# Row maxima of four heads as four 32-row matmul tiles in an attention layer between two ternary feed-forward layers

## The reference

```
x = x + 0.5 * ffn(layernorm(x))       # relu(h @ Wq1.T + b1) @ Wq2.T + b2, 512 hidden, weights in {-1, 0, 1}
x = x + attn(layernorm(x))
x = x + 0.5 * ffn(layernorm(x))
def attn(x):
    q, k, v = heads(x @ Wq.T + bq), heads(x @ Wk.T + bk), heads(x @ Wv.T + bv)
    q, k = rope(q, k)
    return concat(softmax(q @ k.T / sqrt(8)) @ v) @ Wo.T + bo
```

## Time and profile before

| | us |
|---|---|
| Time, median of 3 runs | 548.01 (lowest 547.97) |
| The profiled execution | 545.37 |
| Its span in the profile | 543.5 |
| PE busy | 498.4 (92%) |
| DVE busy | 396.5 (73%) |
| ACT busy | 365.1 (67%) |
| POOL busy | 219.8 (40%) |

### The profile page before, as it was taken

The page is one execution under the profiler, slowest core; times in us unless marked ns, Lnnn a source line. Parts: engine busy times, 40 slices in busy tenths (PEclk is TensorE's granted clock), DMA queues, the critical chain, the costliest instruction groups (busy, mean ns, idle before and its releaser), DMA issues.

```text
span 543.5 us, 8687 instructions
## 1 busy us (share of the span) xinstructions
PE 498.4 (92%) x3230; PEld 234.4 (43%) x3230; DVE 396.5 (73%) x579; ACT 365.1 (67%) x432; POOL 219.8 (40%) x291
## 2 busy tenths in 40 slices
PE   5777988899999999999999999999899999998986
PEld 4455633433444435353535333533344433432445
DVE  3773976768887697768877788778876887888224
ACT  4659866577657685768566866687576757675751
POOL 1553646136554363437351645155513631103202
PEclk7897999999999999999999999999899999999999
DMA  7138026402540247003710444034501470000000
GB/s 225 47 104 240 4 67 190 98 22 98 143 93 2 56 159 159 1 26 114 197 39 6 126 141 103 2 96 154 124 1 50 167 156 2 22 1 3 2 21 19
DMA packets 19177, 44.60 MB, mean 82 GB/s; under 512 B 2624, under 2 KB 5440, under 8 KB 18112
## 3 DMA queue, kind: packets, MB, share of 16 engines
q1 hardware_dynamic: 18464, 43.53, 29.2%
q10 hardware_dynamic: 672, 0.52, 0.3%
HBM read 20.45 MB, written 18.87 MB: 72 GB/s over the span
## 4 chain that ended last, share of the span: by engine, by line
PE 72%; DVE 12%; ACT 10%; issue 3%; DMA 1%; POOL 1%; SPq 0%; ACTq 0%; DVEq 0%; POOLq 0%
PE heads_acc L556 21%; PE unit L541 13%; PE unit L526 11%; PE side L611 8%; DVE maxima L837 8%; ACT probs L747 5%; PE side L594 3%; PE side L599 3%; PE side L605 3%; PE heads_acc L619 2%; ACT hidden L737 2%; PE side L580 2%; DVE x_lo L854 2%; PE unit L611 1%; PE side L590 1%
## 5 line engine op out<-in xcount | busy, mean ns | idle before, releaser
L837 DVE TENSOR_REDUCE maxima<-unit 128x2 f32<-128x1024 f32 x256 | 303.4, 1221 | 72.3 <-PE unit L526 70.7
L747 ACT ACTIVATE probs<-unit 128x1024 f32<-128x1024 f32 x256 | 254.5, 1024 | 99.7 <-PE unit L541 98.3
L556 PE MATMUL heads_acc<-probs,v_heads 128*32 128x512 f32 x1024 | 136.7, 607 | 1.1 <-ACT probs L747 1.1
L541 PE MATMUL unit<-q_stack,k_stack 64*128 64x512 f32 x512 | 113.8, 463 | 8.3 <-DVE maxima L837 4.8
L526 PE MATMUL unit<-k_stack,q_stack 62*128 62x512 f32 x512 | 106.5, 438 | 6.9 <-DVE maxima L837 4.4
L1001 POOL TENSOR_SCALAR max_parts<-maxima 128x16 fp32r<-128x16 f32 x32 | 6.5, 203 | 180.0 <-DVE maxima L837 180.0
L541 PEld LDWEIGHTS unit<-q_stack,k_stack 64*128 64x128 f32 x512 | 46.3, 185 | 74.3 <-DVE maxima L837 30.5
L526 PEld LDWEIGHTS unit<-k_stack,q_stack 62*128 62x128 f32 x512 | 47.4, 185 | 66.7 <-issue 31.9
L611 PE MATMUL side<-w_q,hidden 128*128 128x128 f32 x416 | 53.8, 282 | 0.0
L611 PEld LDWEIGHTS side<-w_q,hidden 128*128 128x128 f32 x416 | 48.5, 191 | 9.5 <-issue 9.3
L737 ACT ACTIVATE hidden<-side,b_col 128x512 f32<-128x512 f32 x49 | 33.8, 689 | 10.2 <-PE side L605 10.1
(11 more groups left out here) (142 smaller groups left out, 480.6 us busy)
## 6 DMA issues: line engine op xcount, KB each, us to landing
k_scratch<-k_parts SPq DMA_DIRECT2D x16, 512.0 KB, 2.9
q_scratch<-q_parts SPq DMA_DIRECT2D x16, 512.0 KB, 3.6
k_stack<-k_scratch SPq DMA_DIRECT2D x14, 512.0 KB, 7.1
q_stack<-q_scratch SPq DMA_DIRECT2D x14, 512.0 KB, 9.0
resid<-in_x SPq DMA_DIRECT2D x8, 256.0 KB, 6.2
k_swap<-k SPq DMA_DIRECT2D x16, 128.0 KB, 2.3
q_swap<-q SPq DMA_DIRECT2D x16, 128.0 KB, 2.3
out_y<-resid SPq DMA_DIRECT2D x7, 256.0 KB, 2.0
```

What stands on the lines that cost most here:

```text
L541: mm = pe.matmul(to[:, e, :], k_stack[part, quad // NQ % 2, pair, kt * P:(kt + 1) * P], q_stack[part, quad // NQ % 2, pair, :], start=True ...
L556: mm = pe.matmul(heads_acc[32 * j:32 * j + 32, :], v_heads[:, b % 2, at, ODD * odd:ODD * odd + 32], probs[:, burst % RING, j, :], start=(k ...
L747: act.activation(probs[:, burst % RING, 2 * pp:2 * pp + 2, :], unit_of(USE_OF["exp", n]), ACT.Exp, scale=SCALE).then_inc(s_exp, 1)
L837: dve.tensor_reduce(maxima[:, quad % 2, :, r], unit_of(USE_OF["max", k]), AX_X, ALU.max).then_inc(s_max, 1)
```

## The change

Four edits go together.

- `m` now takes four heads at a time: four matmuls of 32 rows x 512 columns, at partitions 0, 32, 64 and 96, into two units (four banks). Both units must be free before the first matmul. DVE reduces the two units one after the other. A batch has 16 such `m`, and `LEAD` is 6.
- They read a stack copy of their own, `q_max` and `k_max`: product rows alone, a ring of two half batches (`max_stack`, two DMAs of 512 KB for a half).
- The exponentials' stacks become a ring of three half batches (`E_RING`); `stack` is called for each half, with eight DMAs of 128 KB in place of four of 512 KB for a batch. `set_rows` fills three slots of half the size, 12 calls in place of 8.
- The orders are new, and `qk_order` lays the channels out for the new copies.

The diff, cut to its core (of `PE_FIRST`, and of constants and semaphores, parts are left out):

```diff
-LEAD = 12
+HALVES = 2 * B
+HSTEPS = STEPS // 2
+M_RING = 2
+E_RING = 3
+ALL_BLOCKS = B * NQ * T
+LEAD = 6
...
 PE_STEADY = """
-ffn1_T m e
-heads_copy1@-1 m pv ffn1_up0 e m ffn1_up1
-e m
-e ffn1_stats@5 heads_T1@-1
-e pv m
-e m max_T1 pv ffn1_up2 m
-e m out_T pv ffn1_up3 m
-e
-e out
-e ffn2_stats
-e pv m m ffn1_down0 ffn1_down1 ffn1_down2 m
-e m ffn1_down3 pv
-e max_T2
-e m pv m
-e attn_stats
-e v
-heads_copy0 pv m m pv ffn2_T e m ffn2_up0
-e
-e m ffn2_up1
-e pv heads_T0
-e m m ffn2_up2
-e pv max_T3
-e m m ffn2_up3 pv
-e m ffn2_down0
-e m m ffn2_down1 ffn2_down2 ffn2_down3
-e m
-e pv attn_T
-e m
-e k pv
-e m m pv max_T4
-e m q
-e m pv
+e ffn1_T m
+e pv ffn1_up0
+e
+heads_copy1@-1 ffn1_up1 m e ffn1_stats@5
+e heads_T1@-1 pv
+e m pv max_T1 m ffn1_up2
+e out_T
+e pv ffn1_up3 m
+e pv out
+e m ffn2_stats ffn1_down0 ffn1_down1 ffn1_down2
+e m pv
+e ffn1_down3
+e m
+e pv attn_stats max_T2
+e
+e v
+heads_copy0 m pv pv ffn2_T e m ffn2_up0
+e ffn2_up1
+e
+e pv heads_T0
+e m ffn2_up2
+e pv max_T3
+e m ffn2_up3 pv
+e ffn2_down0 m
+e ffn2_down1 ffn2_down2 ffn2_down3
+e attn_T
+e m k
+e
+e pv m max_T4
+e q
+e pv m
+e pv pv
 """
...
+    if step[0] == "m" and COUNTS["max"] < ALL_BLOCKS:
+        USERS += [("max", 2 * COUNTS["max"] + i) for i in range(2)]
+        COUNTS["max"] += 1
...
-BESIDE_MAX = dict(zip((3, 4, 5, 6), first_ffn("down", 3, 0)))
-BESIDE_MAX_TAKEN = 7
+BESIDE_MAX = dict(zip((1, 2, 3, 4), first_ffn("down", 3, 0)))
+BESIDE_MAX_TAKEN = 4
...
-        q_stack = sb("q_stack", [P, 2, NPAIR, S], F32R)
-        k_stack = sb("k_stack", [P, 2, NPAIR, S], F32R)
+        q_stack = sb("q_stack", [P, E_RING, NPAIR // 2, S], F32R)
+        k_stack = sb("k_stack", [P, E_RING, NPAIR // 2, S], F32R)
+        q_max = sb("q_max", [P, M_RING, 2, S], F32R)
+        k_max = sb("k_max", [P, M_RING, 2, S], F32R)
...
+            def max_stack(half, quads, landed):
+                j, h = divmod(half, 2)
                 for n in "qk":
                     sp.wait_ge(s_scratch[n], (j + 1) * 16 * PARTS)
+                wait(sp, s_scores, (half - M_RING + 1) * 2 * T)
+                for n, tile in (("k", k_max), ("q", q_max)):
+                    products = scratch[n][j % 2].rearrange("q k (d ie g) t -> ie (q k d) (g t)", d=DH, ie=4)
+                    sp.dma_start(tile[:, half % M_RING, quads, :].bitcast(F32).rearrange("p g t -> p (g t)"),
+                                 products[:, :, (2 * h + quads.start) * S:(2 * h + quads.stop) * S]).then_inc(landed, 16)
+
+            def stack(half):
+                j, h = divmod(half, 2)
...
+                wait(sp, s_scoresT, (half - E_RING + 1) * HSTEPS)
                 for e in range(2):
+                    for i in range(2):
+                        for n, tile in (("k", k_stack), ("q", q_stack)):
+                            products = scratch[n][j % 2].rearrange("q k (d i e g) t -> (q k d) i e g t", d=DH, e=2, i=2)
+                            sp.dma_start(tile[64 * e:64 * e + PROD, half % E_RING, i:4:2, :].bitcast(F32),
+                                         products[:, i, e, 2 * h:2 * (h + 1), :]).then_inc(s_stack[half % E_RING], 16)
...
                     to_scratch("q", b + 1)
-                    stack(b + 1, slice(0, NPAIR), s_stack[(b + 1) % 2])
+                    max_stack(2 * b + 2, slice(0, 2), s_max_stack[0])
+                    stack(2 * b + 2)
...
                     max_row((b + 1) * NQ)
+                    max_stack(2 * b + 3, slice(0, 2), s_max_stack[1])
+                    stack(2 * b + 3)
...
+                for i in range(2):
+                    if (free := unit_free(USE_OF["max", 2 * k + i])) is not None:
+                        pe.wait_ge(*free)
+                for i in range(2):
+                    to = unit_of(USE_OF["max", 2 * k + i])
+                    for e in range(2):
+                        tile = 2 * i + e
+                        part = slice(32 * tile, 32 * tile + PROD)
+                        mm = pe.matmul(to[:, e, :], q_max[part, half % M_RING, gl, t * P:(t + 1) * P],
+                                       k_max[part, half % M_RING, gl, :], start=True, stop=True)
                 mm.then_inc(s_scores, 1)
...
-            pe.wait_ge(s_rows_set, 4)
...
-                dve.tensor_reduce(maxima[:, quad % 2, :, r], unit_of(USE_OF["max", k]), AX_X, ALU.max).then_inc(s_max, 1)
+                for i in range(2):
+                    dve.tensor_reduce(maxima[:, quad % 2, :, T * i + t], unit_of(USE_OF["max", 2 * k + i]), AX_X, ALU.max).then_inc(s_max, 1)
...
-    qk_order = np.arange(D).reshape(NPAIR, 2, DH // 2, 2).transpose(3, 2, 1, 0).reshape(-1)
+    qk_order = np.arange(D).reshape(NQ, 2, 2, DH // 2, 2).transpose(4, 3, 1, 2, 0).reshape(-1)
```

More of the change, by code:

```diff
@@ L143, in work @@
         yield from tokens(plan, b)
-USERS = [("max", k) for k in range(LEAD)]
+USERS = [("max", k) for k in range(2 * LEAD)]
 COUNTS = {"max": LEAD, "exp": 0}
 for step in work(PLANS):
[L149 to L153, removed]
+    if step[0] == "e" and COUNTS["exp"] < ALL_STEPS:
+        USERS.append(("exp", COUNTS["exp"]))
+        COUNTS["exp"] += 1
+    if step[0] == "m" and COUNTS["max"] < ALL_BLOCKS:
+        USERS += [("max", 2 * COUNTS["max"] + i) for i in range(2)]
+        COUNTS["max"] += 1
 USE_OF = {user: use for use, user in enumerate(USERS)}
@@ L370, in bank_taken, with max_stacked, stacked @@
                     "ffn1_down": s_x1, "ffn2_down": s_y}[name], index + 1
-        def stacked(j, g):
-            return (s_stack_first, STACK_LANDED) if j == 0 and g == 0 else (s_stack[j % 2], (j // 2 + 1) * STACK_LANDED)
+        def max_stacked(half):
+            return s_max_stack[half % M_RING], (half // M_RING + 1) * M_LANDED
+        def stacked(half):
+            return s_stack[half % E_RING], (half // E_RING + 1) * E_LANDED
         last = B - 1
@@ L477, in _ @@
             to_scratch("q", 0)
-            stack(0, slice(0, 2), s_stack_first)
-            stack(0, slice(2, NPAIR), s_stack[0])
+            max_stack(0, slice(0, 1), s_max_first)
+            stack(0)
+            max_stack(0, slice(1, 2), s_max_stack[0])
+            max_stack(1, slice(0, 2), s_max_stack[1])
+            stack(1)
             max_row(0)
@@ L511, in scores_of @@
             def scores_of(k):
-                if k >= ALL_STEPS:
+                if k >= ALL_BLOCKS:
                     return
-                quad, r = divmod(k, QSTEPS)
-                pair = (quad % NQ) * 2 + r // T
-                t = r % T
-                if r == 0:
-                    pe.wait_ge(*stacked(*divmod(quad, NQ)))
-                    if quad == NQ:
-                        pe.wait_ge(s_rows_set, 8)
-                if (free := unit_free(USE_OF["max", k])) is not None:
-                    pe.wait_ge(*free)
-                to = unit_of(USE_OF["max", k])
-                for e in range(2):
-                    part = slice(64 * e, 64 * e + ROWS_MAX)
-                    mm = pe.matmul(to[:, e, :], q_stack[part, quad // NQ % 2, pair, t * P:(t + 1) * P],
-                                   k_stack[part, quad // NQ % 2, pair, :],
-                                   start=True, stop=True)
+                quad, t = divmod(k, T)
+                half, gl = divmod(quad, 2)
+                if t == 0 and quad == 0:
+                    pe.wait_ge(s_max_first, M_LANDED)
+                elif t == 0:
+                    pe.wait_ge(*max_stacked(half))
+                for i in range(2):
[8 more added lines that the diff above has]
+                                       k_max[part, half % M_RING, gl, :], start=True, stop=True)
                 mm.then_inc(s_scores, 1)
@@ L532, in scores_T_of @@
                 quad, r = divmod(n, QSTEPS)
-                pair = (quad % NQ) * 2 + r % 2
-                kt = r // 2
+                kt, i = divmod(r, 2)
+                half, gl = divmod(quad, 2)
                 if r == 0:
+                    pe.wait_ge(*stacked(half))
+                    if half < E_RING:
+                        pe.wait_ge(s_rows_set, 4 * (half + 1))
                     pe.wait_ge(s_maxrow, (quad + 1) * 32)
@@ L786, in _ @@
             set_rows(1, "q", 1)
+            for e in range(2):
+                set_rows(2, "k", e)
+                set_rows(2, "q", e)
             side_part(("max_T", 0, 0, 0))
```

84 lines of the change are left out of this document (42 added, 42 removed).

## The result

The changed kernel takes **724.4 us** (median of four runs) against 548.0: a ratio of 1.325, 95% interval 1.318 to 1.332. It is slower, as predicted, but the time lies 134 us above the range. Its profiled span is 720.9 us.

What follows compares the result with a forecast made beforehand. PE's own steps were taken as the bound. 404.9 us of steps, 58.6 of ring waits and 14 of other waits gave 477.5 against 452.4; less 1.8, 23.3 more, so 571 us on 548.0; range 555 to 590.

Steps and rivals of the forecast that it cites:

- the part on DMAs: SP's queue: 16 MB more of copies counted as nothing; without cover, late maximum rows would cost 7 us in all.
- The second rival: Blocks of four matmuls dearer on PE, 583 us, or with maximum rows also 7 us late, 590; chance 0.14.
- PE's own time: PE's steps without waits: a block of four matmuls costs 0.433 us; the sum falls by 5.3 to 404.9 us.
- The prediction's own last sign: Profile sign of being wrong: PE waiting for `max_row` or a stack's landing would make the DMAs the story.
- the third: Rival: no price for PE changing between 32- and 64-row shapes, so `m` and `e` share runs; 561 us, chance 0.09.
- the fourth rival: No price between 32 and 64 rows on PE, and the other waits gone; 547 us, chance 0.05.
- The prediction's estimate from the 3.07: By the skill's speedup for four row tiles, a block on PE streams 0.07 us longer; about 576 us.
- The ring's waits: PE waiting for free units in the ring of three: 58.6 us against 28.2 before, 30 us more.
- the prediction's own example: In the steady order, the first `e` behind the block waits 0.23 us and the second 0.80; together 1.03.
- The other 14 us of waits: PE waiting for `hidden`, x_lo or a reduction behind other DVE work; kept at 14 us, bounds nothing to 14 more.
- Ahead of the orders: Start of the kernel: a half-size `set_rows` between two `hidden` on ACT gives 1.8 us back.
- The first rival: The 14 us of PE's other waits fall into the ring's new waits; about 557 us, chance 0.14.

Runs made afterwards that it cites:

- e1_even: The changed kernel with each 512 KB DMA of the maximum copies cut into four of 128 KB, one per 32 partitions; 581.5 us, ratio 1.064 to the kernel before.
- e7_even_half_max: e1_even with each DVE reduction reading half of its unit's columns, exponentials scaled down; 559.7 us, ratio 1.024 to the kernel before.
- e11_even_orders2: e1_even with its written orders drawn up again, counting the waits of all five engines; 556.9 us, ratio 1.021 to the kernel before.
- e6_before_rows4: The kernel before with product rows reordered and each stack DMA in two of 16 rows, outermost dimension 4; 615.7 us beside 544.6.
- e5_outer2: The changed kernel with each DMA of the maximum copies cut into two of 64 partitions, outermost dimension 2; 862.5 us.

## Why the prediction was wrong

**The step that failed is the part on DMAs: "I count nothing; without that cover an `e` would wait, by 1 us a batch if the small DMA lands behind the 2 MB, 7 us in all."** It cost some 143 us (724.4 less 581.5). The step counted issues, bytes and the slack of `max_row`. It took the speed of the new DMAs from old ones that land 512 KB in 9.0 us, and these have 32 product rows outermost; the new pattern, with 4, stands in the diff. So the cover was counted with 16 engines where four worked. The second rival had half of the mechanism, rows that come late, at a twentieth of the size, and the range ended with it. The other half it had not: PE stood for 49.5 us ahead of blocks whose own copy had not landed, beside 53.6 ahead of `e` (47.7 under "issue", 5.9 put down to `max_row`). And the stalls took the clock with them: from the first to the last `e`, PE's own time is 472.8 us for 431.8 in e1_even (table). The prediction's own last sign, PE waiting for `max_row` or a stack's landing, is what the profile shows.

The Trainium skill has the rule: the page "DMA: Bandwidth & Descriptors", section Why a DMA increments its semaphore by 16 and not by 1, says that a DMA uses the largest number of engines up to 16 that divides the slowest dimension of both of its patterns. The traces agree: 0.25 of the engines at 4 steps, 0.13 at 2, about 1.0 at 32, and no change where the outer 4 merges with the next dimension.

- *PE's own time* was right. A block costs 0.44, and entry and exit are paid beside the 64-row pairs as beside any other shape (a pair and a block in a row, between other steps: 211.06, 211.49, 211.93 below, 0.43 and 0.44); that excludes the third and the fourth rival (0.23) and the dear blocks of the second. The prediction's estimate from the 3.07 of the Trainium skill, "TensorE: Matmul & The Clock Gate", section Measured speedup vs the span model, was a block of 0.50; these rows don't show it.
- *The ring's waits* were right in kind. PE's timeline of e1_even at the prediction's own example, `m e e heads_T pv e`:

```profile
205.73 0.51 PE L560 MATMUL unit<-k_max,q_max 32*128 32x512 f32 x4
206.28 0.50 PE L577 MATMUL unit<-q_stack,k_stack 64*128 64x512 f32 x2
207.58 0.79 PE L577 MATMUL unit<-q_stack,k_stack 64*128 64x512 f32 x2 [0.80 <-DVE maxima L876]
208.30 1.11 PE L616 MATMUL side<-ident_f,heads 128*128 128x128 f32 x4
209.34 1.79 PE L592 MATMUL heads_acc<-probs,v_heads 128*32 128x512 f32 x8
211.06 0.50 PE L577 MATMUL unit<-q_stack,k_stack 64*128 64x512 f32 x2
211.49 0.51 PE L560 MATMUL unit<-k_max,q_max 32*128 32x512 f32 x4
211.93 1.07 PE L592 MATMUL heads_acc<-probs,v_heads 128*32 128x512 f32 x8
```

  The idle time ahead of the second `e` is the 0.80 of the prediction, and that `e` starts 1.85 after the block (said: about 1.8). In all, PE's idle time ahead of `e` and `m` that ended with DVE or ACT is 42.9 us in e1_even (the groups shown under e7_even_half_max) and 12.8 in the kernel before:

```profile
L541 PE MATMUL unit<-q_stack,k_stack 64*128 64x512 f32 x512 | 113.8, 463 | 8.3 <-DVE maxima L837 4.8 <-ACT probs L747 2.1
L526 PE MATMUL unit<-k_stack,q_stack 62*128 62x512 f32 x512 | 106.5, 438 | 6.9 <-DVE maxima L837 4.4 <-ACT probs L747 1.5
```

  That is 30.1 more, and the prediction said 30. Both levels lie 15 to 16 us under its 58.6 and 28.2, so it had the difference right and not the levels; why, no run shows. Without the badly dealt DMAs the forecast of 571 is some 10 us short.
- *A term was missing: the clock.* The same rows go on with 1.04 for the transposes (208.30 to 209.34) and 1.72 for `pv`, where 0.58 and 1.00 were counted. Windows of e1_even around them:

```profile
204.00:207.00 3.00, 2.37 (x12) 0.68 (x10) 2.38 (x3) 2.48 (x4) 0.00 (x0) 1.00 1.09 217
207.00:211.00 4.00, 3.42 (x14) 1.20 (x14) 3.48 (x12) 2.23 (x3) 2.10 (x4) 0.57 0.97 321
```

  After the waits the granted clock lies at its lower level, 1.2 GHz, for most of 4 us. It does not always fall there: one batch earlier the same wait is followed by full speed, and one batch later too (271.23).

```profile
145.37 0.51 PE L577 MATMUL unit<-q_stack,k_stack 64*128 64x512 f32 x2 [0.80 <-DVE maxima L876]
145.80 0.66 PE L616 MATMUL side<-ident_f,heads 128*128 128x128 f32 x4
```

  Steady batches at 1.00 take 62.2 (one stands under e1_even), as the prediction named. Longer than named are a steady batch at 0.97 and a late one, for which it named 59, at 0.92:

```profile
200.60:264.20 63.60, 59.44 (x388) 26.00 (x384) 46.35 (x67) 42.13 (x52) 29.82 (x40) 0.97 0.44 113
326.40:388.60 62.20, 55.29 (x344) 22.62 (x340) 44.05 (x57) 39.02 (x47) 24.29 (x33) 0.92 0.44 114
```

  Over the whole stretch of the orders the clock is 0.96 in e1_even's profile, a run of 585.4 us, and 1.00 before (table): 0.04 x 488 = 20 us' worth of clock pulses, some of them in idle time. PE's own time shows what of it counts: 431.8 us for 427.3, 4.5 more where the sum had 5.3 less, so about 10 us by this estimate, the size of the gap. How much exactly, no run separates.
- *The other 14 us of waits* were kept as they were. (They are 15: the 452.4 runs from start to start and leaves out the last `pv`, which the 410.2 counts, in both kernels alike.) No run shows them by themselves.
- *Ahead of the orders* 1.8 us were to be gained. The first `e` starts at 72.0 in e1_even and at 71.9 before: nothing was.
- *The first rival* (557) would need waits that fall together. e11_even_orders2 comes to that time by other orders, which says that the waits can be had, not that they fell away by themselves.

## What to carry to other kernels

Before a DMA is counted as hidden, read the outermost dimension of both of its patterns, after merging: here 4 steps meant a quarter of the engines, and both the big DMA and the small one queued behind it stopped the compute. A shape that takes two buffers of a ring of three in one step has to save more on its engine than the ring takes back; here 5 us, as reckoned, stood against 30, as measured. An order made for one kind of wait moves the time to the next one; counted over all engines it was worth 2% to the old kernel and 4% to e1_even (581.5 to 556.9).

## What the runs showed of the hardware

- Four DMA engines alone moved 61 to 106 GB/s and two 52, up to 26 GB/s each; all 16 together, in loads of the stacks and copies, moved 217 to 222, 14 each. By the packet records a packet of 16 KB took 0.61 us in e6_before_rows4 (240 to 248) and 1.26 in the kernel before (208 to 212). A few engines by themselves are so not as slow as their number says, which is where e6_before_rows4's expectation went wrong. The 14 hold for these loads only: a stretch of e1_even with `to_scratch` (207 to 211) moved 321.
- Behind the badly dealt copies SP's issues take longer, 2.97 us for a DMA of 128 KB in the changed kernel where 0.4 to 0.6 is usual, and here in e5_outer2, on SP's timeline:

```profile
320.12 5.56 SPq L490 DMA_DIRECT2D k_stack<-k_scratch  x1
```

- Idle time of 0.80 us, with some shorter waits just ahead of it, was followed by the lower clock for about 3.5 us in one batch of e1_even (207.58 to 211.06), where the wait itself was the smaller part of the price, and by the full clock in the batches beside it (145.37 and 271.23). After the stalls of 8.21 and 6.16 us in the changed kernel the same matmuls took 0.80 in place of 0.50.
